# A layer norm's gain and shift taken from its transposed copy through TensorE, with its row sums on ScalarE, in a pipelined Mamba and mixture-of-experts kernel

## What is computed

```python
m = _mamba(x, ...)                                   # state scan: h = dA*h + dt*B*u ; y = h . C
h = _layernorm(m + x, ln0_g, ln0_b)
q = gelu(_l2norm(h @ q_w.T + q_b, -1))
k = _l2norm(h @ k_w.T + k_b, -1)
qw = q @ w_g * D_MODEL ** (-0.5)
Aw = _l2norm(qw, 1)
G = (Aw * q).sum(1)
hs = G[:, None, :] * k @ proj_w.T + proj_b
hs = hs * _layernorm(h, lni_g, lni_b) @ fl_w.T + fl_b
h2 = _layernorm(hs + h, ln1_g, ln1_b)
f = gelu(h2 @ d1_w.T + d1_b) @ d2_w.T + d2_b
out = _layernorm(f + h2, ln2_g, ln2_b)
...
x = x + _layernorm(out)
x = x + _layernorm(experts(_layernorm(x)))
```

## Time and profile before

| | us |
|---|---|
| median of 3 runs | 5962.66 (5957.35 to 5971.64) |
| profiled execution | 5962.0 |
| its span, first to last instruction | 5960.1 |
| mean granted TensorE clock | 0.959 |
| TensorE busy | 5312.1 (89%) |
| VectorE busy | 4968.6 (83%) |
| GpSimd busy | 4274.7 (72%) |
| ScalarE busy | 3795.7 (64%) |

### The profile page before, as it was taken

One profiled execution on the slowest core, in us unless ns is written; L12 is line 12 of the kernel. 1 busy time (PEld: TensorE's weight loads), 2 busy tenths in 40 slices (PEclk: granted clock), 3 DMA queues, 4 the chain that ended last, 5 costly groups with the idle time before them and its releaser, 6 DMA issues. The chain is left out here.

```text
span 5960.1 us, 73233 instructions
## 1 busy us (share of the span) xinstructions
PE 5312.1 (89%) x17952; PEld 3035.6 (51%) x17952; DVE 4968.6 (83%) x6468; ACT 3795.7 (64%) x6464; POOL 4274.7 (72%) x2941
## 2 busy tenths in 40 slices
PE   5799999999999999999999999999999998759990
PEld 2355555555555555555555555555555555536660
DVE  5999999999999999999999999999999999512226
ACT  5667777777777677776776777777676776311114
POOL 3678777877787777777777777887777777514447
PEclk8999999999999999999999999999999999879995
DMA  7877777777677776766766766666666666315556
GB/s 230 297 263 246 239 241 243 246 237 240 236 241 237 237 241 234 239 233 237 241 234 232 237 233 234 230 230 234 226 232 226 230 228 235 105 36 128 121 114 232
DMA packets 485923, 1316.15 MB, mean 221 GB/s; under 512 B 54911, under 2 KB 194816, under 8 KB 485392
## 3 DMA queue, kind: packets, MB, share of 16 engines
q1 hardware_dynamic: 441264, 1242.26, 62.3%
q0 software_dynamic: 30720, 34.17, 3.2%
q10 hardware_dynamic: 13408, 34.08, 1.5%
HBM read 1189.54 MB, written 138.02 MB: 223 GB/s over the span
## 5 line engine op out<-in xcount | busy, mean ns | idle before, releaser
L543 POOL TENSOR_TENSOR st<-st,C_rows 128x1024 f32<-128x1024 f32 x1024 | 2455.5, 2410 | 475.2 <-DVE st L1156 474.2
L1156 DVE TENSOR_TENSOR_SCAN st<-dA,drive 128x1024 f32<-128x1024 f32 x1024 | 2335.6, 2281 | 142.3 <-ACT dA L753 82.6
L933 PE MATMUL y<-st,ident 128*128 128x512 f32 x4096 | 1974.8, 618 | 173.0 <-POOL st L543 170.2
L753 ACT ACTIVATE dA<-delta,a_neg 128x511 f32<-128x511 f32 x2048 | 1363.4, 713 | 436.7 <-DVE st L1156 405.0
L933 PEld LDWEIGHTS y<-st,ident 128*128 128x128 f32 x4096 | 771.2, 196 | 1123.6 <-issue 780.6
L1129 DVE TENSOR_TENSOR drive<-du,B_rows 128x1024 f32<-128x1024 f32 x1024 | 1258.3, 1229 | 97.5 <-DVE du L1124 21.7
L902 PE MATMUL pre_bank<-e_abs,in_w 128*128 128x512 f32 x1024 | 479.4, 601 | 48.9 <-ACT g L707 39.2
L1039 PE MATMUL post_bank<-d_w,gT 128*128 128x256 f32 x2048 | 491.7, 384 | 26.4 <-issue 25.6
L1039 PEld LDWEIGHTS post_bank<-d_w,gT 128*128 128x128 f32 x2048 | 382.6, 193 | 130.6 <-issue 87.5
L1459 POOL DMA_INDIRECT token_rows<-O,dest_i x128 | 197.6, 1544 | 307.6 <-DVE O L1506 223.2
L625 POOL DMA_INDIRECT expert_in<-tb,idx x256 | 256.4, 1002 | 154.5 <-DVE idx L1298 81.2
(11 more groups left out here) (215 smaller groups left out, 8092.7 us busy)
## 6 DMA issues: line engine op xcount, KB each, us to landing
B_rows<-bc_rows SPq DMA_DIRECT2D x1024, 512.0 KB, 3.7
C_rows<-bc_rows SPq DMA_DIRECT2D x1024, 512.0 KB, 5.0
expert_in<-zeros ACTq DMA_DIRECT2D x22, 768.0 KB, 7.5
X<-expert_in SPq DMA_DIRECT2D x32, 528.0 KB, 4.9
xin<-in_x SPq DMA_DIRECT2D x32, 512.0 KB, 6.4
xn_rows<-xin SPq DMA_DIRECT2D x32, 512.0 KB, 5.6
token_rows<-zeros SPq DMA_DIRECT2D x32, 512.0 KB, 8.1
h<-xn_rows SPq DMA_DIRECT2D x32, 512.0 KB, 6.6
```

The source lines that it names most:

```text
L543: pool.tensor_tensor(tile[:, :, :], tile[:, :, :], bc[1][k % ROWS[1]][:, :, :], ALU.mult)\
L753: return act.activation(dA[k % 2][:, j, 1:L], delta[par][:, c, 1:L], ACT.Exp, scale=a_neg[:, c, n:n + 1])
L933: last = pe.matmul(Y[:, :], ident[:, :], st[k % RING][:, j, :], start=False, stop=pair == CU - 1 and j == 1)
L1156: dve.tensor_tensor_scan(st[k % RING][:, :, :].rearrange("p a l -> p (a l)"), dA[k % 2][:, :, :].rearrange("p a l -> p (a l)"), DR[:, :, : ...
```

## The change

h with gain and shift is no longer made on GpSimd. When `F` holds the transposed, scaled and shifted copy, TensorE transposes it back into the post banks (`hB`, eight transposes), and ScalarE copies the banks to h and makes the row sums with the same instructions (`hi_sum`). The sums of squares follow on ScalarE (`hi_sq`, its copy goes to `li`), and GpSimd makes mean, scale and shift from them (`hi_m`, then `scale_of`). VectorE's statistics of h are gone, and so are the rows `ln0_g` and `ln0_b`. `q` now waits for `hi_sum`, since it writes the same banks, and `q_sq` for `hi_sq`, since both use `li`. Most slots in the tuples are new, on all engines and in all stages.

```diff
-                ("q_b", "pr_b", "fl_b", "ln0_g", "ln0_b", "lni_g", "lni_b", "ln2_g", "ln2_b", "w_g")}
+                ("q_b", "pr_b", "fl_b", "lni_g", "lni_b", "ln2_g", "ln2_b", "w_g")}
...
+        sum_hi = sb("sum_hi", [P, TT])
+        sq_hi = sb("sq_hi", [P, TT])
...
 SyncE    pre
-                at = iter((0, 56, 71, 73, 95, 95))
+                at = iter((2, 58, 73, 76, 92, 93))
 SyncE    post
-                at = iter((5, 67))
+                at = iter((30, 91))
 SyncE    late
-                at = iter((41, 59))
+                at = iter((56, 58))
 GpSimd   pre
-                at = iter((9, 11, 76, 76, 84, 93))
+                at = iter((7, 15, 76, 76, 88, 93))
 GpSimd   post
-                at = iter((10, 28, 32, 35, 39, 45, 51, 52, 56, 62, 62, 73))
+                at = iter((15, 24, 33, 33, 42, 44, 50, 61, 63, 63, 75))
                 yield next(at)
                 pool.wait_ge(*post_dve.at("h_aggr", b))
                 scale_and_shift(post_pool, "h", r, shift, mv, EPS, b)
                 yield next(at)
-                pool.wait_ge(*post_pe.at("hT", b))
-                times("h_g", h, rows["ln0_g"])
-                yield next(at)
-                pool.wait_ge(*post_pool.at("h_g", b))
-                plus("h_b", h, rows["ln0_b"])
+                pool.wait_ge(*post_act.at("hi_sum", b))
+                mean_of(post_pool, "hi", shift, sum_hi)
+                yield next(at)
+                pool.wait_ge(*post_act.at("hi_sq", b))
+                scale_of(post_pool, "hi", r, shift, sq_hi, EPS, b)
                 yield next(at)
                 pool.wait_ge(*post_act.at("q_sq", b))
                 power(post_pool, "q", rq, ssq[:, :], EPS * EPS, ALU.max, b)
-                yield next(at)
-                pool.wait_ge(*post_dve.at("hi_aggr", b))
-                scale_and_shift(post_pool, "hi", r, shift, mv, EPS, b)
 GpSimd   late
-                at = iter((26, 30, 32, 33, 34, 46, 47, 47, 47, 50, 50, 50, 50))
+                at = iter((21, 22, 26, 33, 36, 46, 47, 48, 50, 52, 54, 54, 54))
 ScalarE  pre
-                at = iter((5, 13, 13, 25, 25, 32, 38, 44, 46, 46, 51, 52, 58, 60, 60, 62, 65, 65, 67, 67, 67, 68, 80, 95))
+                at = iter((7, 15, 20, 20, 21, 28, 32, 41, 43, 43, 48, 56, 56, 61, 64, 64, 67, 69, 70, 71, 71, 74, 86, 92))
 ScalarE  post
-                at = iter((16, 27, 35, 38, 42, 43, 46, 54, 66, 73, 75, 85, 92, 92, 92))
+                at = iter((20, 24, 25, 27, 28, 36, 36, 36, 42, 50, 65, 73, 75, 82, 91, 92, 92))
...
+                act.wait_ge(*post_pe.at("hB", b))
+                for tile in range(TT):
+                    last = act.activation(h[:, tile, :], tiles_in(PB)[tile], ACT.Identity, accum_out=sum_hi[:, tile:tile + 1])
+                last.then_inc(post_act.did("hi_sum"), 1)
+                yield next(at)
+                act.wait_ge(*post_pool.at("hi_m", b))
+                act.wait_ge(*post_act.at("hi_sum", b))
+                squares_of(lambda tile: li[:, tile, :], h, shift, sq_hi).then_inc(post_act.did("hi_sq"), 1)
+                yield next(at)
                 act.wait_ge(*post_dve.at("q_sum", b))
+                act.wait_ge(*post_act.at("hi_sq", b))
 ScalarE  late
-                at = iter((28, 34, 34, 38, 39, 43))
+                at = iter((27, 28, 32, 38, 42, 43))
 TensorE  pre
-                at = iter((22, 26, 29, 36, 44, 45, 51, 51, 51, 53, 57, 59, 60, 60))
+                at = iter((18, 21, 23, 31, 38, 42, 50, 50, 51, 55, 57, 57, 64, 65))
 TensorE  post
-                at = iter((7, 7, 7, 7, 29, 29, 29, 38, 38, 49, 53, 56, 56, 67, 69, 69, 78, 80, 80, 80, 82, 86, 88, 95, 95))
+                at = iter((0, 0, 0, 7, 23, 25, 27, 27, 29, 31, 48, 51, 57, 58, 65, 66, 67, 79, 80, 80, 82, 83, 87, 93, 95,
+                           95))
...
                 turn(h, PB).then_inc(post_pe.did("hT"), 1)
+                yield next(at)
+                pe.wait_ge(*post_act.at("hT", b))
+                for tile in range(TT):
+                    for c in range(KD):
+                        last = pe.transpose(PB[tile // 2][:, (tile % 2) * D + c * P:(tile % 2) * D + (c + 1) * P],
+                                            F[:, c, tile * P:(tile + 1) * P], ident[:, :])
+                last.then_inc(post_pe.did("hB"), 1)
                 for tile in range(TT):
                     if tile % 2 == 0:
                         yield next(at)
                     if tile == 0:
-                        pe.wait_ge(*post_act.at("hT", b))
+                        pe.wait_ge(*post_act.at("hi_sum", b))
                     last = token_major(F, q_w, KD, tile)
 TensorE  late
-                at = iter((0, 10, 10, 16, 16, 16, 17, 18, 39, 41, 46))
+                at = iter((0, 0, 2, 6, 12, 12, 14, 14, 43, 46, 50))
 VectorE  pre
-                at = iter((30, 31, 36, 39, 40, 41, 43, 45, 95, 95, 95))
+                at = iter((27, 28, 33, 35, 37, 38, 41, 44, 95, 95, 95))
 VectorE  gates
-                at = iter((29, 51, 75))
+                at = iter((31, 54, 75))
 VectorE  post
-                at = iter((0, 9, 11, 32, 34, 37, 49, 49, 52, 60, 71, 71))
+                at = iter((0, 11, 14, 29, 46, 46, 49, 62, 71, 71))
...
-                dve.wait_ge(*post_pool.at("h_b", b))
-                yield from stats(post_dve, "hi", tiles_of(h), stat, mv, b, at)
-                yield next(at)
 VectorE  late
-                at = iter((23, 23, 25, 26, 27, 28, 41, 41, 42, 42, 45, 45))
+                at = iter((20, 20, 22, 23, 25, 25, 43, 44, 45, 45, 46, 46))
```

More of the change, by code:

```diff
@@ L283, in attention_phase @@
         scan_du = Steps(sem("scan_du"), range(KI))
-        post_pe = Steps(sem("post_pe"), ["m0", "m1", "m2", "m3", "hT", "q", "k", "ssk", "G", "hs", "tT", "fl", "sT"]
+        post_pe = Steps(sem("post_pe"), ["m0", "m1", "m2", "m3", "hT", "hB", "q", "k", "ssk", "G", "hs", "tT", "fl", "sT"]
                         + [f"d1_{j}" for j in range(KF)])
         late_pe = Steps(sem("late_pe"), [f"d2_{tile}" for tile in range(TT)] + ["nT", "dots", "cum"])
-        post_act = Steps(sem("post_act"), ["h_normed", "hT", "q_sq", "kT", "k_sq", "li_n", "q_gelu", "G", "proj_g", "tT", "s_normed", "sT"]
+        post_act = Steps(sem("post_act"), ["h_normed", "hT", "hi_sum", "hi_sq", "q_sq", "kT", "k_sq", "li_n", "q_gelu", "G", "proj_g", "tT", "s_normed", "sT"]
                          + [f"gelu{j}" for j in range(KF)])
@@ L290, in attention_phase @@
         post_dve = Steps(sem("post_dve"), ["h_stats", "h_aggr", "q_sum"]
-                         + ["hi_stats", "hi_aggr", "qw", "qw2", "ssk", "ssg", "t",
+                         + ["qw", "qw2", "ssk", "ssg", "t",
                             "s_stats", "s_aggr"])
@@ L297, in attention_phase @@
                             "slot0", "slot1", "idx"])
-        post_pool = Steps(sem("post_pool"), ["h_m", "h_v", "h_r", "h_shift", "h_g", "h_b", "q_v", "q_r", "hi_m", "hi_v", "hi_r", "hi_shift", "li_g", "li",
+        post_pool = Steps(sem("post_pool"), ["h_m", "h_v", "h_r", "h_shift", "hi_m", "hi_v", "hi_r", "hi_shift", "q_v", "q_r", "li_g", "li",
                                              "G_v", "G_r", "k_v", "k_r", "h_fl", "t_li", "s_m", "s_v", "s_r", "s_shift"])
```

## The result

The changed kernel takes **6019.77 us** (median of 4 runs, 6013.69 to 6026.35), the kernel before 5965.42 beside it (4 runs): ratio **1.0085 [1.0070, 1.0101]**. It is slower by 0.85 per cent, and above the range. Its profiled run took 6026.35 us, its span is 6024.6.

What follows compares the result with a forecast made beforehand. VectorE was taken as the bound, TensorE right beside it. Per sequence -1.2 (work) - 2.9 (old waits) + 1.2 + 0.4 + 0.4 (new waits) = -2.1 us; with 30, 5962.7 - 63 = 5900 us, range 5830 to 5985.

Steps and rivals of the forecast that it cites:

- VectorE is the engine that sets the time: In the steady loop VectorE works 148.4 of 159.0 us a sequence and is seldom starved, with TensorE right beside it.
- VectorE's 1.2 us less work: Dropping VectorE's statistics and aggregations of h saves 1.2 us a sequence, with 0 and 2.24 as ends.
- The 2.9 us of old waits: Of VectorE's 3.3 us a sequence waiting for ScalarE's decays and for `fl` at `s_stats`, 2.9 go.
- fl at 66 and 67 ends the wait of `s_stats`: With `s_stats` still at slot 71, VectorE's wait there for the `fl` product, 0.7 us a sequence, should end.
- the new hole after k=16 of my last sentence: The forecast fails if the order after scan step 16, followed least closely, opens a new wait; no size given.
- 1.2 us at scan 4: At the sequence's start VectorE waits 1.1 to 1.2 us for TensorE's first add, delayed by more `d2` work.
- just done: `h_stats`, moved to slot 11 about 14.7 us in, finds the last `m` tile done at 14.9, so no wait was counted.
- The 0.4 each for `f_stats` and `dots`: New VectorE waits for TensorE: 0.4 us a sequence at `f_stats`, and 0.4, up to 0.8, at `dots`.
- SyncE's two steps of cover: Two steps (7.4 us) cover the B and C row loads behind SyncE's wait for the scatters, so no cost.
- TensorE's 1.08: The eight added fp32 transposes cost TensorE 8 x 0.135 = 1.08 us a sequence.
- The starved scans 10 to 12: Case, chance 0.10: ScalarE's block delays decays for scans 10 to 12, another 2 us of waits, about 5963 us.
- The last, 6023: Case, chance 0.14: TensorE becomes the bound, in head and bank chain; +2.0 us a sequence, 6023 us.

Runs made afterwards that it cites:

- early_c10: The change on nearly the order of the kernel before, with GpSimd's mean of `n_h` also moved behind the state product of scan 10: 5952.7 us, ratio 0.9983.
- before_decay: The kernel before, without the change, with ScalarE's `G` moved from slot 54 to 55 and VectorE's `t` from 60 to 62: 5964.8 us, ratio 0.9995.
- rk: The changed kernel with GpSimd's power for k moved from slot 61 to 51: 6014.3 us, ratio 1.0082.
- d2_less: The changed kernel with seven products of the first `d2` tile's second half left out on TensorE in the head: 5974.3 us, ratio 1.0013.
- one_back: The changed kernel with seven of the eight transposes of `hB` left out: 6018.7 us, ratio 1.0091.
- old_places: The change's operations at the slots of the kernel before, the new ones placed between them: 6152.1 us, ratio 1.0311.

## Why the prediction was wrong

The forecast was -2.1 us a sequence, the result is +2.1. VectorE's work fell by 0.6 in place of 1.2, and its idle time rose by 2.7 where the sum had it fall by 0.9. The step that failed is "VectorE is the engine that sets the time": the sum took a VectorE wait removed for time won, and priced new ones one by one in VectorE's queue.

- **VectorE's 1.2 us less work: nearly right where nothing more is stretched** (1.0 in early_c10), 0.6 in the changed kernel: `dv` grew by 0.68 us, `du` by 0.33, while the row products of `qw`, stretched before, got 0.74 shorter. That an instruction's duration depends on its neighbour on another engine was not in the sum.
- **The 2.9 us of old waits: 2.2 gone, and worth nothing. Here the step failed.** Decays: 2.6 became 0.4. I had asked what ends each wait, not which engine is full while it lasts. before_decay removes the largest of them and its ratio is 0.9995 [0.9986, 1.0004].
- **"fl at 66 and 67 ends the wait of `s_stats`": wrong.** 0.7 became 0.8; `tT` waits for `t_li`, which waits for `t` and `rk`. `rk` at slot 61 I had priced at nothing: VectorE waited 1.97 us for it at k=20, and 1.12 at the third gate behind it. That is the new hole after k=16 of my last sentence. Moving it alone (rk) won nothing either.
- **The head: 1.2 us at scan 4 was right (1.23 measured), the stretch was not.** `h_stats`, "just done", waited another 0.8, all of it in the 11 of 25 sequences whose first `d2` tiles ran at the lower clock level after TensorE's pause; I had summed these products at the higher one. d2_less shows that this is the dearest place. The 0.4 each for `f_stats` and `dots` did not come.
- **SyncE's two steps of cover** held only behind the late `rk`; without it (rk) the rows were 2.1 us late.
- **TensorE's 1.08: right** (27.3 us for 200, so 1.09), and in the changed kernel free (one_back). But TensorE was busy 3.0 us more, not 1.1: `fl` (+1.2 us) and the in-projections (+1.0) fell into stretches at the lower clock level. These cover 8.5 us a sequence in place of 4.5, and begin in most sequences at k=15 or 16 and again at k=21 or 22, before the change only at k=20 or 21.
- **ScalarE:** the copies took 383 ns, so 1.5 us for four, just under the bounds (1.6 to 2.2); added work 4.8 for 5.0. The starved scans 10 to 12 did not come in the new order. In the old one the block sat on TensorE (old_places).
- **The cases.** The last, 6023 (the paragraph on TensorE calls it the fourth; it is the fifth), has the measured time, by half of its mechanism, and that it is only 3 us off is luck: TensorE is the bound in the head, but by more work and a lower clock, while its waits fell (9.9 to 9.0). Its place was half right too, since the bank chain cost nothing. Its chance, 0.14, was too small; a row that shows TensorE at 34.00 of 34 us where more of its work was to be placed should have made it the first.

## What to carry to other kernels

A mean share of 93% on two engines hides stretches where one of them is at 100%: look at windows of 20 to 40 us, and give nothing for a wait of the other engine inside such a stretch. Before moving GpSimd's work, list VectorE's steps with two inputs in SBUF and see which of them it will meet. The same operations gave +3.1%, +0.9% and -0.2% on three orders, and the best is the old order with few moves, not the one that was new throughout. Even there 1.0 us less VectorE work a sequence made it only 0.3 us shorter, so count work taken off one engine as won only where no other is full.
